# Sparse-layer front with half-width convolution matmuls and rows shared with GpSimd, and a transposing add in the recurrent layer, in a four-layer block on one core

## The chip, the cores and the metric

One core of a Trainium2 chip runs the whole program. The metric is the device time of one execution, in microseconds (us), lower is better. The engines are named as the profile names them: PE is TensorE, DVE is VectorE, ACT is ScalarE, POOL is GpSimd, SP is SyncE (here it only issues DMAs). PEld is TensorE's weight load.

## The reference

The input `x` is 4 batches of 1024 rows of 256 numbers, so 4096 rows, all in float32. Four layers are added to it in turn, each on a layer-normalised copy of `x`:

```python
x = x + lru(layernorm(x))        # linear recurrent unit
x = x + ffn(layernorm(x))        # sparse feed-forward layer
x = x + attention(layernorm(x))  # 8 heads, latent keys and values
x = x + ffn(layernorm(x))        # the same sparse layer, same weights
```

Of the recurrent unit the last part matters here: `out` is its output before a small two-layer net, and it computes `y = gelu(out @ w1 + b1) @ w2 + b2 + out`, then a layer norm of `y`.

The sparse layer needs two gates (`so` and `si`). Each gate begins with what the reference calls a convolution: the 256 normalised columns are taken in 64 groups of 4, and each group is reduced to one number with its own 4 weights.

```python
xc = einsum('ngf,gf->ng', x2d.reshape(n, 64, 4), conv_w) + conv_b   # n = 4096 rows
mean, var = over all n rows                                          # batch norm
xa = gelu((xc - mean) * rsqrt(var + eps) * gamma + beta)
scores = softmax(xa @ lin_w.T + lin_b)    # then the top 32 of 256 are kept
```

The mean and variance run over all 4096 rows, so nothing behind them can begin before the last row's convolution is done. That part, from the normalised rows to the batch-norm statistics, is what is called the front of a sparse layer below.

## The kernel before

All 4096 rows of `x` stay in the on-chip memory. The work before the batch norm goes in 8 chunks of 512 rows, each of 4 tiles of 128 rows; the work behind it goes in 32 tiles. Each engine has its own program, written out by hand in the order in which it runs; engines meet only at semaphores.

**A chunk of a front.** (1) ACT writes four normalised tiles with one multiply-add each (`z_rows_of`, line 755), into one of two row buffers. (2) PE turns them by eight 128x128 transposes (`transposes`, line 1522) into two PSUM banks. (3) ACT copies the two banks to `zT` (`zT_chunk`, line 762), so that the 256 columns now lie on 2 x 128 partitions. (4) PE multiplies with the matrix `conv` (`feature_chunk`, line 1553): 256 inputs to 128 outputs, 64 of each gate, as two matmuls of 128x128 weights and 512 columns that add up in one bank. (5) DVE adds the bias into `xcT` (line 1303) and takes statistics (line 1306). The scale and shift of a row's norm (`rs`) come from DVE's statistics and four small POOL instructions (`next_rstd`, lines 576 to 584). `conv` is mostly zeros: the first 128 columns of a row feed only the first 32 groups of each gate, the other 128 only the last 32.

The first sparse layer's front (f = 0) is woven into the last two steps of the recurrent layer; its last chunk needs the last residual of that layer. The second one's front (f = 1) stands by itself behind the attention layer, in `ffn(1)` of ACT, PE, POOL and DVE.

**A step of the recurrent layer** (`lru_step`, 8 of them) runs on PE in a fixed order: input products, transposes two chunks ahead, the mixing matmuls (line 1574), more input products (line 1535), `w1` (line 1589), input products again, and then the `w2` group (lines 1602 and 1604): for each of 4 tiles, two matmuls of 256 columns with `w2`, and then `out` is added to the same sums by two ordinary matmuls with the identity, which turn it back to rows. The group waits for both halves of the gelu (`l_y1`, ACT line 831):

```python
for k in range(KB2):
    mm(o, y1T[:, k, js], w2[:, k, :], start=k == 0, stop=False)
for k in range(KB2):
    last = mm(o[:, k * P:k * P + P], outT2[:, k, js], ident[:, :], start=False,
              stop=k == KB2 - 1)
```

**Set-up.** SP issues the weights' DMAs one after another (line 486), then the other chunks of `x` (line 490). POOL spreads the convolution's weights into a masked array (line 603), DVE sums it to `conv` (line 1296), and ACT copies the turned gate weights into `lin` (lines 798 and 799).

## Time and profile before

| | |
|---|---|
| median of 3 runs | 1435.57 us (1435.55 to 1437.32) |
| profiled execution, own time | 1435.77 us |
| profiled execution, span | 1434.1 us |
| PE busy | 1236.0 us (86%) |
| DVE busy | 1185.6 us (83%) |
| ACT busy | 1104.1 us (77%) |
| POOL busy | 982.3 us (69%) |

The span reaches from the first to the last instruction of the program; 1.7 us of the execution lie around it. PE's busy time overstates its work, since a matmul's record includes the time in which its results drain; for the rate of a series of matmuls one takes the distance of their starts. A float32 matmul of the program is two MATMUL records, a float32 transpose is one. The recurrent layer with the woven-in front takes the first 296 us, the sparse layer behind it runs to about 500 us, attention to 1204 us, and the second sparse layer to the end.

### The profile page before, as it was taken

The numbers are of one execution on the slowest core, as the hardware profiler recorded it, in microseconds if no ns is written. First come the engines' busy times: TensorE is split into PE (matmuls) and PEld (weight loads), VectorE is DVE, ScalarE is ACT, GpSimd is POOL, SyncE is SP. The second block draws the span as 40 slices with busy tenths as digits, with TensorE's granted clock in tenths as the row PEclk, the third lists the DMA queues.
The fourth block names the chain that finished last, engine by engine and source line by source line (L and its number), as shares of the span: only waits on it lengthen the run. The fifth ranks groups of instructions, "written<-read, shape, count | busy, mean of one in ns | idle before, by whom it ended". The sixth has DMA issues, their size and how long they took to land.

```text
span 1434.1 us, 31009 instructions
## 1 busy us (share of the span) xinstructions
PE 1236.0 (86%) x10236; PEld 762.0 (53%) x10236; DVE 1185.6 (83%) x3173; ACT 1104.1 (77%) x2487; POOL 982.3 (69%) x1109
## 2 busy tenths in 40 slices
PE   3899999866777688999999999999999999677775
PEld 2455545434444435565666666666666667344443
DVE  6999999469999978777887778877778853699997
ACT  3232332678899769999999998999998986898886
POOL 4355753248788867777777677777777771288887
PEclk9899999969899999999999999999999999899998
DMA  7100000000000000000000000000000000000000
GB/s 196 44 1 1 1 0 1 0 1 1 1 1 1 1 1 2 2 3 2 2 2 3 2 2 1 3 2 2 2 2 2 2 2 1 0 16 31 21 25 30
DMA packets 26427, 14.84 MB, mean 10 GB/s; under 512 B 14422, under 2 KB 26012, under 8 KB 26268
## 3 DMA queue, kind: packets, MB, share of 16 engines
q1 hardware_dynamic: 26268, 12.87, 3.4%
q8 instruction: 82, 1.34, 0.4%
q14 instruction: 77, 0.63, 0.1%
HBM read 8.60 MB, written 4.19 MB: 9 GB/s over the span
## 4 chain that ended last, share of the span: by engine, by line
PE 47%; DVE 19%; issue 16%; ACT 13%; POOL 4%; DVEq 0%; DMA 0%; SPq 0%; POOLq 0%; ACTq 0%
PE banks L1821 6%; PE banks L1823 5%; PE banks L1810 5%; DVE arena L1364 5%; ACT arena L1035 4%; DVE arena L1359 4%; PE banks L1771 3%; PE banks L1747 3%; PE banks L1839 3%; PE banks L1838 3%; PE banks L1840 3%; PE banks L1574 3%; ACT arena L1043 2%; POOL arena L713 2%; PE banks L1553 2%
## 5 line engine op out<-in xcount | busy, mean ns | idle before, releaser
L713 POOL TENSOR_TENSOR arena<-arena 128x512 f16<-128x512 f32 x384 | 441.1, 1166 | 156.5 <-ACT arena L1043 151.8
L1035 ACT ACTIVATE arena<-banks 128x512 f32<-128x512 f32 x512 | 304.5, 600 | 53.5 <-PE banks L1823 49.8
L1438 DVE TENSOR_REDUCE arena<-banks 128x1 f32<-128x512 f32 x512 | 327.4, 680 | 8.9 <-PE banks L1810 5.9
L1043 ACT ACTIVATE arena<-arena 128x512 f16<-128x512 f32 x512 | 316.2, 633 | 0.0
L1838 PE MATMUL banks<-arena 128*128 128x65 f16 x2048 | 214.4, 193 | 6.2 <-POOL arena L713 5.8
L1839 PE MATMUL banks<-arena 128*128 128x64 f16 x2048 | 214.5, 195 | 0.0
L1840 PE MATMUL banks<-arena 128*128 128x65 f16 x2048 | 213.6, 192 | 0.0
L1838 PEld LDWEIGHTS banks<-arena 128*128 128x128 f16 x2048 | 190.9, 96 | 35.4 <-issue 9.4
L1462 DVE TENSOR_TENSOR arena<-arena 128x512 f16<-128x512 f32 x128 | 106.5, 832 | 124.7 <-ACT arena L1043 124.3
L1364 DVE MATCH_REPLACE8 arena<-arena 128x256 f32<-128x256 f32 x512 | 205.7, 409 | 1.1 <-issue 0.8
L1821 PE MATMUL banks<-arena 128*128 128x512 f16 x512 | 194.1, 379 | 14.3 <-ACT arena L1035 12.8
L1839 PEld LDWEIGHTS banks<-arena 128*128 128x128 f16 x2048 | 190.2, 97 | 28.3
L1359 DVE MAX8 arena<-arena 128x8 f32<-128x256 f32 x512 | 190.2, 413 | 14.1 <-ACT arena L879 9.6
L1810 PE MATMUL banks<-arena 128*128 128x512 f16 x512 | 193.8, 380 | 4.6 <-DVE arena L1438 4.6
L1823 PE MATMUL banks<-arena 128*128 128x512 f16 x512 | 193.8, 378 | 0.0
L1840 PEld LDWEIGHTS banks<-arena 128*128 128x128 f16 x2048 | 190.3, 99 | 0.0
L1699 PE MATMUL banks<-fW,arena 128*128 128x256 f32 x256 | 79.8, 438 | 42.2 <-ACT arena L926 42.2
L1810 PEld LDWEIGHTS banks<-arena 128*128 128x128 f16 x512 | 57.8, 113 | 71.3 <-DVE arena L1438 11.9
L1821 PEld LDWEIGHTS banks<-arena 128*128 128x128 f16 x512 | 50.4, 98 | 58.0 <-ACT arena L1035 35.9
L1699 PEld LDWEIGHTS banks<-fW,arena 128*128 128x128 f32 x256 | 46.4, 201 | 61.8 <-ACT arena L926 57.7
L1686 PE MATMUL banks<-fW,arena 128*128 128x256 f32 x256 | 79.0, 439 | 0.0
L1678 PE MATMUL banks<-lin,arena 128*128 128x512 f32 x128 | 72.6, 651 | 4.8 <-ACT arena L951 4.8
(197 smaller groups left out, 2670.0 us busy)
## 6 DMA issues: line engine op xcount, KB each, us to landing
x<-in_L_attn_a_x SPq DMA_DIRECT2D x8, 512.0 KB, 3.9
out<-x SPq DMA_DIRECT2D x8, 512.0 KB, 2.9
arena<-arena SPq DMA_DIRECT2D x64, 1.0 KB, 1.9
arena<-in_L_attn_a_W_in SPq DMA_DIRECT2D x1, 768.0 KB, 5.7
arena<-in_L_attn_a_W_mid SPq DMA_DIRECT2D x1, 512.0 KB, 7.5
arena<-in_L_attn_a_w_w SPq DMA_DIRECT2D x2, 256.0 KB, 8.0
arena<-in_L_attn_b_Wq SPq DMA_DIRECT2D x1, 512.0 KB
arena<-in_L_attn_b_Wo SPq DMA_DIRECT2D x1, 512.0 KB
```

Source lines behind the costliest of these rows:

```text
L713: nc.gpsimd.tensor_tensor(pr_lo[c][:, kt, :], pr[:, kt, :], pr_hi[c][:, kt, :], ALU.subtract).then_inc(a_lP, 1)
L1035: nc.scalar.activation(pr[:, kt, :], ps[6 + kt % 2][:, :], ACT.Exp, scale=SM_SCALE).then_inc(a_P, 1)
L1043: nc.scalar.activation(pr_hi[c][:, kt, :], pr[:, kt, :], ACT.Copy).then_inc(a_hi, 1)
L1359: nc.vector.max(m8[p][:, i, r, :], src).then_inc(f_k[i], 1)
L1364: nc.vector.match_replace(wk[p][:, i, r % 2, :], m8[p][:, i, r, :], src, TAKEN).then_inc(f_k[i], 1)
L1438: nc.vector.tensor_reduce(mx_half[c][:, i // 2, i % 2:i % 2 + 1], ps[n % MAX_BANKS][:, :], X, ALU.max).then_inc(a_mx, 1)
L1810: mm(ps[n % MAX_BANKS][:, :], every[:, j, :], kA[B % 2][:, half * CH:half * CH + CH], start=True, stop=True).then_inc(a_mps, 1)
L1821: mm(o[:, :], kA[B % 2][:, kt * P:kt * P + P], qA[:, slot, c * CH:c * CH + CH], start=True, stop=False)
L1823: mm(o[:, :], kB[B % 2][:, kt * P:kt * P + P], qB[:, slot, c * CH:c * CH + CH], start=False, stop=True).then_inc(a_sps, 1)
L1838: mm(o, pr_hi[c][:, kt, js], lat[B % 2][:, kt, 0:1 + HD], start=kt == 0, stop=False)
L1839: mm(o[:, 1:1 + HD], pr_hi[c][:, kt, js], lat[B % 2][:, kt, 1 + HD:], start=False, stop=False)
L1840: last = mm(o, pr_lo[c][:, kt, js], lat[B % 2][:, kt, 0:1 + HD], start=False, stop=kt == KT - 1)
```

## The change

Three edits and what goes with them.

1. **Convolution.** The outputs are laid out anew: partitions 0 to 63 hold groups 0 to 31 of both gates, partitions 64 to 127 groups 32 to 63. `conv` becomes two blocks of 64 columns. Instead of two 128-column matmuls that add up, there are two matmuls with 64 weight columns, one per half of the inputs, each writing its own half of the bank's partitions. With the layout go the weights' DMAs (4 and 12 small ones for 2 and 6), the masked array (128 columns for 256), and ACT's copies into `lin` (4 for 2 per half).
2. **Rows.** In the whole second front and in the last two chunks of the first, ACT writes two of the four normalised tiles and POOL the other two (`half_rows`); PE waits for both (`s_zh`).
3. **Recurrent layer.** `out` is added by transposing matmuls (`is_transpose=True`) into the running sums, between the two `w2` matmuls of a tile, and PE waits for the second half of the gelu only before the first tile's second `w2` matmul.

```diff
-        conv = sb("conv", [P, KB2, P])
+        conv = sb("conv", [P, KB2, HD])
...
+        QUAD = HD // 2
...
-            (lin_n[:, :, 0:HD], so_lin_w.rearrange("(k p) g -> p k g", p=P)),
-            (lin_n[:, :, HD:P], si_lin_w.rearrange("(k p) g -> p k g", p=P)),
-            (bnp[0:HD, 0:1], so_conv_b.rearrange("(g a) -> g a", a=1)),
...
+        ] + [(lin_n[:, :, QUAD * q:QUAD * q + QUAD],
+              (so_lin_w, si_lin_w)[q % 2].rearrange("(k p) g -> p k g", p=P)[:, :, QUAD * (q // 2):QUAD * (q // 2) + QUAD])
+             for q in range(4)] + [
+            (bnp[QUAD * q:QUAD * q + QUAD, i:i + 1],
+             pair[q % 2].rearrange("(g a) -> g a", a=1)[QUAD * (q // 2):QUAD * (q // 2) + QUAD, :])
+            for i, pair in enumerate(((so_conv_b, si_conv_b), (so_gamma, si_gamma), (so_beta, si_beta)))
+            for q in range(4)
...
+            def half_rows(of, dst, turns):
+
+                pool.wait_ge(s_tps, turns)
+                for j in (2, 3):
+                    last = nc.gpsimd.tensor_scalar(dst[:, j, :], x[:, of * TPC + j, :], rs[:, of * TPC + j, 0:1],
+                                                   rs[:, of * TPC + j, 1:2], ALU.mult, ALU.add)
+                last.then_inc(s_zh, 1)
+
             over_chunks(pool, lru_step)
             rstd2(NCH - 1)
             residual(NCH - 1)
+            pool.wait_ge(n_p, 4 * (NCH - 1))
+            half_rows(NCH - 2, front_row[0], 2 * (LN_FFN1 + NCH - 3))
...
             next_rstd((NCH - 1) * TPC, NCH - 1, TPC)
+            pool.wait_ge(n_p, 4 * NCH)
+            half_rows(NCH - 1, front_row[1], 2 * (LN_FFN1 + NCH - 2))
             ffn(0)
...
-            for chunk in range(NCH - 3, NCH):
-                rstd_of("out", chunk)
+            for n in range(NCH):
+                if n == 2:
+                    rstd_of("out", NCH - 3)
+                    rstd_of("out", NCH - 2)
+                if n == 4:
+                    rstd_of("out", NCH - 1)
+                pool.wait_ge(n_p, 4 * group_of["out", n] + 4)
+                half_rows(n, z_rows[n % 2], 2 * (LN_FFN2 + n - 1) if n > 1 else 2 * LN_FFN2)
...
-                z_rows_of(m, front_row[m % 2])
+                z_rows_of(m, front_row[m % 2], 2 if m >= NCH - 2 else TPC)
...
-                for k in range(KB2):
-                    last = mm(ps[xc_bank(f, n)][:, :], conv[:, k, :], zT[n % 2][:, k, :], start=k == 0,
-                              stop=k == KB2 - 1)
+                for k in range(KB2):
+                    last = mm(ps[xc_bank(f, n)][HD * k:HD * k + HD, :], conv[:, k, :], zT[n % 2][:, k, :],
+                              start=True, stop=True)
...
-                pe.wait_ge(l_y1, n * 2 + 2)
+                pe.wait_ge(l_y1, n * 2 + 1)
...
+                    mm(o, y1T[:, 0, js], w2[:, 0, :], start=True, stop=False)
                     for k in range(KB2):
-                        mm(o, y1T[:, k, js], w2[:, k, :], start=k == 0, stop=False)
-                    for k in range(KB2):
-                        last = mm(o[:, k * P:k * P + P], outT2[:, k, js], ident[:, :], start=False,
-                                  stop=k == KB2 - 1)
+                        mm(o[:, k * P:k * P + P], outT2[:, k, js], ident[:, :], start=False, stop=False,
+                           is_transpose=True)
+                    if j == 0:
+                        pe.wait_ge(l_y1, n * 2 + 2)
+                    last = mm(o, y1T[:, 1, js], w2[:, 1, :], start=False, stop=True)
```

How instructions stand on PE in a `w2` group and in the woven-in front behind it (names: `arena` holds the recurrent layer's and the row buffers, `zrow` is the other row buffer). Before, two of the four tiles of the last group and what follows:

```order
L1602 MATMUL banks<-arena 128x256 x2
L1604 MATMUL banks<-ident,arena 128x128 x2
L1602 MATMUL banks<-arena 128x256 x2
L1604 MATMUL banks<-ident,arena 128x128 x2
L1522 MATMUL banks<-ident,zrow 128x128 x8
L1553 MATMUL banks<-zT,conv 128x512 x2
L1522 MATMUL banks<-ident,arena 128x128 x8
```

Now:

```order
L1624 MATMUL banks<-arena 128x256
L1626 MATMUL banks<-ident,arena 128x128 x2
L1630 MATMUL banks<-arena 128x256
L1624 MATMUL banks<-arena 128x256
L1626 MATMUL banks<-ident,arena 128x128 x2
L1630 MATMUL banks<-arena 128x256
L1543 MATMUL banks<-ident,zrow 128x128 x8
L1576 MATMUL banks<-zT,conv 64x512 x2
L1543 MATMUL banks<-ident,arena 128x128 x8
```

The two turning matmuls now stand between the two `w2` matmuls, and the convolution's two matmuls write 64 partitions each; the number of operations is the same.

POOL's program at the end of the recurrent layer (L564, now L565, is the last residual; L576 to L584, now L577 to L585, is `next_rstd` of the last chunk). Before:

```order
L564 TENSOR_TENSOR x<-x,arena 128x1024
L576 TENSOR_TENSOR nve<-nmv,eps_c 128x4
L577 TENSOR_TENSOR nnm<-nmv,minus_one 128x4
L581 TENSOR_TENSOR rs<-nve,minus_half 128x4
L584 TENSOR_TENSOR rs<-nnm,rs 128x4
L638 TENSOR_SCALAR bn_var<-bmv 128x1
```

Now:

```order
L565 TENSOR_TENSOR x<-x,arena 128x1024
L635 TENSOR_SCALAR zrow<-x,rs 128x256 x2
L577 TENSOR_TENSOR nve<-nmv,eps_c 128x4
L578 TENSOR_TENSOR nnm<-nmv,minus_one 128x4
L582 TENSOR_TENSOR rs<-nve,minus_half 128x4
L585 TENSOR_TENSOR rs<-nnm,rs 128x4
L635 TENSOR_SCALAR arena<-x,rs 128x256 x2
L649 TENSOR_SCALAR bn_var<-bmv 128x1
```

The rows of chunk 6 stand ahead of the last chunk's scale and shift, those of chunk 7 behind them. In the second front POOL writes two tiles for each of the 8 chunks, with the last chunk's scale and shift between chunks 3 and 4:

```order
L635 TENSOR_SCALAR zrow<-x,rs 128x256 x2
L635 TENSOR_SCALAR arena<-x,rs 128x256 x2
L577 TENSOR_TENSOR nve<-nmv,eps_c 128x4
L578 TENSOR_TENSOR nnm<-nmv,minus_one 128x4
L582 TENSOR_TENSOR rs<-nve,minus_half 128x4
L585 TENSOR_TENSOR rs<-nnm,rs 128x4
L635 TENSOR_SCALAR zrow<-x,rs 128x256 x2
```

Before, POOL had the three chunks' scales and shifts there and nothing else.

## Rows read from the trace of the kernel before

**Rows 1.** The page: busy time of the engines

```profile
PE 1236.0 (86%) x10236; PEld 762.0 (53%) x10236; DVE 1185.6 (83%) x3173; ACT 1104.1 (77%) x2487; POOL 982.3 (69%) x1109
```

**Rows 2.** Timeline, DVE: start, length, operation, [idle before, who ended it]

```profile
99.38 1.41 DVE L1206 SCALAR_TENSOR_TENSOR arena<-banks,arena 128x512 f32<-128x512 f32 x2 [0.34 <-PE banks L1535]
101.02 1.41 DVE L1206 SCALAR_TENSOR_TENSOR arena<-banks,arena 128x512 f32<-128x512 f32 x2 [0.23 <-PE banks L1535]
...
168.74 1.78 DVE L1296 TENSOR_REDUCE conv<-xcT 128x64 f32<-128x256 f32 x4
```

**Rows 3.** Timeline, PE, last four steps of the recurrent layer

```profile
186.65 3.67 PE L1535 MATMUL banks<-zT,arena 128*128 128x512 f32 x8 [2.03 <-DVE arena L1206]
...
242.08 1.13 PE L1602 MATMUL banks<-arena 128*128 128x256 f32 x4 [0.78 <-ACT arena L831]
243.05 0.61 PE L1604 MATMUL banks<-ident,arena 128*128 128x128 f32 x4
243.49 1.03 PE L1602 MATMUL banks<-arena 128*128 128x256 f32 x4
...
258.61 1.88 PE L1553 MATMUL banks<-zT,conv 128*128 128x512 f32 x4
260.33 1.04 PE L1522 MATMUL banks<-ident,zrow 128*128 128x128 f32 x8
261.20 1.02 PE L1589 MATMUL banks<-arena 128*128 128x512 f32 x2
...
267.64 1.07 PE L1522 MATMUL banks<-ident,arena 128*128 128x128 f32 x8 [1.11 <-ACT arena L755]
```

**Rows 4.** Timeline, POOL, then PE and DVE, end of the first front

```profile
279.13 2.00 POOL L564 TENSOR_TENSOR x<-x,arena 128x1024 f32<-128x1024 f32 x1 [2.56 <-ACT arena L776]
283.73 0.20 POOL L576 TENSOR_TENSOR nve<-nmv,eps_c 128x4 f32<-128x4 f32 x1 [2.61 <-DVEq L1156]
...
288.66 5.30 PE L1553 MATMUL banks<-zT,conv 128*128 128x512 f32 x8
...
280.36 0.75 DVE L1303 TENSOR_SCALAR xcT<-banks,bnp 128x512 f32<-128x512 f32 x1 [2.13 <-PE banks L1553]
...
281.75 1.39 DVE L1142 BATCH_NORM_STATS2 nst<-x 128x6 f32<-128x256 f32 x4
```

**Rows 5.** Timeline, ACT, PE and DVE, second front

```profile
1206.26 2.06 ACT L755 ACTIVATE zrow<-x,rs 128x256 f32<-128x256 f32 x4
1208.23 1.06 ACT L762 ACTIVATE zT<-banks 128x512 f32<-128x512 f32 x2
1209.18 2.07 ACT L755 ACTIVATE arena<-x,rs 128x256 f32<-128x256 f32 x4
...
1204.14 1.04 PE L1522 MATMUL banks<-ident,zrow 128*128 128x128 f32 x8
...
1227.72 0.75 DVE L1303 TENSOR_SCALAR xcT<-banks,bnp 128x512 f32<-128x512 f32 x1 [0.24 <-PE banks L1553]
```

**Rows 6.** Two stretches: length, busy of PE, PEld, DVE, ACT, POOL, granted clock

```profile
288.60:294.00 5.40, 5.40 (x13) 2.26 (x10) 1.46 (x3) 1.88 (x4) 0.00 (x0) 0.68 0.00 0
1205.40:1228.00 22.60, 22.45 (x90) 11.79 (x90) 11.63 (x22) 20.54 (x44) 1.56 (x4) 1.00 0.00 1
```

**Rows 7.** Groups by shape, POOL: the one-input operations: busy, mean ns of one

```profile
L683 POOL TENSOR_SCALAR arena<-arena 64x512 f16<-64x512 f16 x64 | 49.1, 767 | 5.3
...
L596 POOL TENSOR_SCALAR arena<-arena 128x512 f32<-128x512 f32 x2 | 4.0, 2010 | 0.1
```

**Rows 8.** Timeline, PE, set-up: 16 records in two partition halves

```profile
41.93 2.22 PE L1642 MATMUL banks<-arena 64*64 64x256 f32 x16
```

**Rows 9.** Timeline, SP, POOL and PE, set-up

```profile
17.66 0.60 SPq L486 DMA_DIRECT2D bnp<-in_L_ffn_si_beta  x1
...
28.86 1.57 POOL L603 TENSOR_SCALAR_AFFINE_SELECT xcT<-xcT 128x256 f32<-128x256 f32 x4
...
60.61 2.08 PE L1574 MATMUL banks<-arena 128*128 128x512 f32 x2 [5.29 <-DVE arena L1240]
```

More of the change, by code:

```diff
@@ L253, in hybrid_block_kernel @@
         s_z = sem("s_z")
+        s_zh = sem("s_z_half_chunk_pool")
         s_tps = sem("s_zT_psum")
@@ L602, in _ @@
                 for i in range(2):
-                    nc.gpsimd.affine_select(out=cvs[:, k, i, :], in_=cvb[:, i, :],
-                                            compare_op=ALU.is_equal, fill=0.0, base=-P * k,
-                                            pattern=[[1, D]], channel_multiplier=-1).then_inc(s_prep, 1)
+                    nc.gpsimd.affine_select(out=cvs[:, k, i, :], in_=cvb[:, i, k * P:k * P + P],
+                                            compare_op=ALU.is_equal, fill=0.0, base=0,
+                                            pattern=[[1, P]], channel_multiplier=-1).then_inc(s_prep, 1)
             add_ln_bias(0)
@@ L748, in _, with z_rows_of @@
             nc.scalar.activation(trig, ang_n, ACT.Sin).then_inc(s_act0, 1)
-            def z_rows_of(of, dst):
+            def z_rows_of(of, dst, rows=TPC):
                 act.sem_inc(s_turn, 1)
-                for j in range(TPC):
+                for j in range(rows):
                     t = of * TPC + j
@@ L797, in _ @@
                 act.wait_ge(s_pe0, k + 1)
-                nc.scalar.activation(lin[0:HD, k * P:k * P + P], ps[4 + k][0:HD, 0:P], ACT.Copy)
-                nc.scalar.activation(lin[HD:P, D + k * P:D + k * P + P], ps[4 + k][HD:P, 0:P],
-                                     ACT.Copy).then_inc(s_ev0, 1)
+                for q in range(4):
+                    at = slice(QUAD * q, QUAD * q + QUAD)
+                    last = nc.scalar.activation(lin[at, D * (q % 2) + k * P:D * (q % 2) + k * P + P],
+                                                ps[4 + k][at, 0:P], ACT.Copy)
+                last.then_inc(s_ev0, 1)
             for k in range(KB2):
@@ L1295, in conv_matrix @@
                 for k, i in ((0, 0), (0, 1), (1, 0), (1, 1)):
-                    link(nc.vector.tensor_reduce(conv[:, k, i * HD:i * HD + HD],
+                    link(nc.vector.tensor_reduce(conv[:, k, i * QUAD:i * QUAD + QUAD],
                                                  cvs[:, k, i, :].rearrange("p (g f) -> p g f", f=4), X, ALU.add))
@@ L1542, in front_turn @@
                     pe.wait_ge(f_xc, m - 1)
+                if m >= NCH - 2:
+                    pe.wait_ge(s_zh, m - NCH + 3)
                 transposes(LN_FFN1 + m, front_row[m % 2], 2 * (m % 2))
@@ L1709, in ffn @@
                     for n in range(2):
+                        pe.wait_ge(s_zh, 3 + n)
                         transposes(LN_FFN2 + n, z_rows[n], 2 * n)
@@ L1713, in ffn @@
                         if n + 2 < NCH:
+                            pe.wait_ge(s_zh, 5 + n)
                             transposes(LN_FFN2 + n + 2, z_rows[n % 2], 2 * (n % 2))
```

13 lines of the change are left out of this document (4 added, 9 removed).

## The prediction

> **What bounds the kernel now.** The page's busy times come first: PE 86%, DVE 83%, ACT 77%, POOL 69% [rows 1]. No engine carries the whole span, so each stage is read by itself, for the wait that ends last there. POOL is the least busy, but in the recurrent layer it writes residuals and scales that others wait for.
>
> The timelines of the recurrent layer show two regimes. In the first four steps PE finds DVE busy: it stands idle 2.03 us for `L1206` at 186.65 [rows 3], and of PE DVE waits only 0.34 and 0.23 us a step [rows 2]. From there PE runs nearly without a gap, so in the last four steps its instructions are the time.
>
> At the end of that layer the chain is serial: the last convolution of DVE's queue, `L1303` at 280.36, stands ahead of the last chunk's statistics, `L1142` at 281.75, and those ahead of POOL's scale and shift at 283.73 [rows 4]. The last two convolutions then run at a clock of 0.68 on average between 288.6 and 294 (a mix of 2.4 and 1.2 GHz) and take 5.30 us for eight records [rows 4, 6].
>
> The second front is ACT-bound in a steady beat: rows 2.06 us, copies 1.06 us, one chunk start to the next 1209.18 - 1206.26 = 2.92 [rows 5]. PE follows at granted clock 1.00 [rows 6]. PE is near its own limit there: eight transposes and four convolution records.
>
> **The transposing add.** A pair of 256-column `w2` matmuls (four records) takes about 0.87 us, the four 128-column records of the identity 243.49 - 243.05 = 0.44 [rows 3]. A transpose is one record: eight take 261.20 - 260.33 = 0.87, so 0.109 each [rows 3]. Two in place of four records save 0.22 a tile, 0.87 a group of four tiles. Steps 4 to 7: 4 x 0.85 = 3.4 (a little taken off for changes of mode). Steps 0 to 3 are DVE's, where PE's lead is worth only what DVE waits for it, 0.34 + 0.23 = 0.57 in all [rows 2]. Sum 4.0. No row shows a transpose into a running sum. Its bounds are 0.109 (a plain one) and 0.22 (no saving); I take 0.109, since nothing in the rows makes a transpose's time depend on its bank.
>
> **The split wait.** PE stands idle 0.78 for the gelu's second half at 242.08 [rows 3]. Now the first half and the tile's turning matmuls (0.43 + 0.22) stand ahead of it, which cover nearly all: 0.7. Behind the wait stand only the rest of the group and the chunks after it, which wait now as well.
>
> **The convolution, in halves.** A chunk takes 260.33 - 258.61 = 1.72, four records of 0.43 [rows 3]. The new matmuls have as many columns, so the count of records is the same; time falls only if the two, on separate column halves of the array, run side by side. The nearest row is `L1642` in set-up: 16 records of 256 columns on 64x64 parts in 2.22 us, where 16 x 0.87 / 4 = 3.5 would be their time one by one [rows 3, 8]. Side by side here: 2 x 0.43 = 0.86, and I put 0.3 on top for two changes between full and half tiles (an estimate; bounds 0 and 0.6): 1.16, saving 0.56.
>
> What that is worth, chunk by chunk: the first two lie on PE's path, 1.1. The third's gain goes into the wait for ACT's rows behind it, 1.11 [rows 3]. The next ones hide behind ACT, but for the sixth: DVE's `L1303` waits 2.13 for it and `L1142` stands behind, so 0.5 (more is held back by POOL's residual, which ends at 281.13) [rows 4]. The last two drop from 5.30 to about 3.9: two pairs at the slow clock and two changes; 1.4. The sum over the bias row `conv`, `L1296`, takes 4 x 0.43 on DVE in the DVE-bound part, and reads half as much: about 0.5 of 1.78 [rows 2].
>
> **POOL's rows.** `half_rows` issues two 128x256 operations with a scale and a shift per partition. No row shows it. The nearest is `L596`, also float32 with a per-partition scalar, but 512 columns: 2.01 us [rows 7]. Its small fixed part is about 0.2 (the 128x4 operation at 283.73 [rows 4]), so by columns 256 take 0.2 + 0.9 = 1.1. The lower bound is `L683`, with constants and half the partitions, 0.77 for 512 columns, so 0.48; the upper is `L596`'s whole 2.01 [rows 7]. I take **1.1**, by the row that is nearest in kind.
>
> In the first front: chunk 6's rows start after the residual (281.13) and end about 281.2 + 2.2 + 0.1 = 283.5, and the last scale and shift, which would now be due at 283.2, come 0.3 late. Chunk 7's take 2.2 + 0.1 for its hand-over, where ACT took 2.06 for four: a loss of 0.2. ACT's two end at 1.0, unused. Together -0.5.
>
> Sum of the first front and the recurrent layer: 4.0 + 0.7 + 1.1 + 0.5 + 1.4 + 0.5 - 0.5 = **7.7**.
>
> The Trainium skill speaks to this price ("GPSIMD Engine Reference", § 3.1): an elementwise loop at about 1.8 cycles an element at best, 769 ns for 512 elements. `L683` agrees, 767 ns; `L596`, 2010 ns for as many, doesn't. By the page a row costs about 0.4 us and the total would come out some 4 us lower, about 1420.
>
> **The second front.** ACT now has 2 x 0.52 + 1.06 = 2.1 a chunk, PE 0.87 + 1.16 + a little = 2.1, POOL 2 x 1.1 = 2.2. So POOL sets the beat, narrowly. Chunks 0 and 1 are written before attention ends; chunk 2's rows need the first chunk's transposes done, 1204.14 + 0.87 + hand-over = 1205.2 [rows 5]. Six chunks from there take 13.2, the last scale and shift between them 1.7 (a 1.0 us power and small ones), to 1220.1. Then the last transposes 1.0, copies 1.1 and convolution 1.2: DVE's last bias at about 1223.6 against 1227.72 [rows 5]. Gain **4.1**. The new wait `s_zh` stands on PE ahead of each chunk's transposes; behind it wait the previous chunk's convolution and DVE's add, which the times above include.
>
> **Set-up, nothing.** SP issues eight more small DMAs at 0.60 [rows 9], 4.8 us, so the last weights come about 28, POOL's `L603` (28.86 now) up to some 2 us later, the other chunks of `x` 4.8 later, and ACT has four copies more, about 1. PE has 5.29 idle before 60.61, for DVE [rows 9]; that is the cover. Gone, it would cost up to 2; and POOL's later work may meet other DVE work: 1 either way.
>
> Together 7.7 + 4.1 = 11.8. The sum is made against the profiled execution's 1435.77 (span 1434.1 plus 1.7), 0.2 over the median: **1424.0**.
>
> **Rivals.**
>
> *The halves do not overlap* (the change does not do what it says). For: both read the same 128 input rows with different moving data, which `L1642`'s 64-row parts don't. A chunk then takes 1.72 + 0.3 = 2.0. In the first front the 3.0 of the convolution become about -0.7; in the second PE's beat is 0.87 + 2.0 = 2.9, as now, minus 0.5 at the edges. 1435.8 - 4.0 + 0.5 = 1432.3.
>
> *POOL's row costs 2.0*, with the price per instruction, not per column: **slower**. Place: the six chunks of the second front (12 operations) and four operations' worth in the first, so 16 us lost for each us of price over 1.1; the change is even at 1.1 + 11.8 / 16 = 1.84. At 2.01 it is 1424.0 + 14.6 = 1438.6. Against: `L683` and the 128x4 rows show that time goes with columns. For: `L596` is the only row of this kind.
>
> *POOL's row costs 0.5.* The beat falls to PE's 2.1 and scale and shift no longer count: 2.1 less; the last chunk of the first front 1.3 and chunk 6's 0.3 less: about 1420.4.
>
> *The clock falls in the second front.* The clock is 1.00 there, but 0.68 at the end of the first front [rows 6], where PE had waited between its chunks. With POOL as bound, PE waits a little in each beat. At 1.2 GHz the transposes 1.74 and the pairs 1.9 make a beat of 3.7, and the second front loses 5.7 where it gained 4.1: 1433.8. The Trainium skill has a rule on that ("TensorE: Matmul & The Clock Gate", Part 4): transposes in transpose mode don't count as busy for the clock. By that rule the shorter convolutions leave less that counts; in the trace, 64 transposes between 32 convolution records kept 1.00, so it has not decided there so far.
>
> *The transposing add is a two-pass operation*: 3.4 less, 1427.4.
>
> **How the numbers follow.** Chances: forecast, with POOL's price from 0.8 to 1.5, 0.50; POOL cheap 0.16; no overlap 0.12; transposing add 0.04; POOL at 2.0 0.08; clock 0.05; other, both signs, 0.05. The likeliest gives **1424.0**; its own range is 1420.5 to 1430.5 (16 us for each us of the price up to 1.5, less of it down to 0.8, where PE bounds the beat; changes of mode 0 to 0.6 and set-up 1 lie within). The range to hold 8 in 10 goes from the cheap POOL to the halves in series, 1419.5 to 1432.5; outside are the slower clock, the expensive row and the unnamed. 0.2% is 2.9 us, about what a measurement of this kernel tells from no change. Faster by more (below 1432.7): 0.50 + 0.16 + 0.04 + most of no overlap, 0.10, and 0.03 of the rest: **0.83**. Same: 0.02 + 0.05 + 0.02 + 0.01 at the even point of POOL's price: **0.10**. Slower: **0.07**.
>
> **What would show it.** In the profile after: the tile of `w2` 1.1 us for 1.31; the convolution's pair 1.2 a chunk, two records starting nearly together; POOL's row 1.1; in the second front a beat of 2.2 with PE's idle time ended by POOL's rows; no clock below 1.00 there; the start of attention some 7.7 us earlier. The forecast is wrong if PE's transposes there wait on ACT or follow without a gap (POOL cheap), if four convolution records still take 1.7 or more, if the beat is over 2.9, or if the first steps of the recurrent layer start later than they did.

## The result and the profile after

The changed kernel takes **1421.35 us**, median of 4 runs (1419.80 to 1424.02), where the kernel before took 1436.44 (4 runs, 1435.55 to 1437.54): ratio 0.9897, 95% interval 0.9877 to 0.9916, so 15 us less (12 to 18). The forecast was 1424.0, range 1419.5 to 1432.5, faster with 0.83. The profiled execution is the fastest of the four, 1419.80 with a span of 1418.1. It is set against the profiled one before, of 1435.77: 16.0 less.

The page of the changed kernel; PE's busy time is 17 us less, POOL's 10 more [rows 1]:

```profile
PE 1219.2 (86%) x10172; PEld 746.1 (53%) x10172; DVE 1183.4 (83%) x3173; ACT 1094.3 (77%) x2471; POOL 992.4 (70%) x1129
```

**Where the 16 us came from.** DVE issues the same 3173 instructions in the same order in both kernels, so its starts can be laid side by side. Five stretches cover the span; each is the difference of two starts (the ends of it are DVE's first `SCALAR_TENSOR_TENSOR` of the recurrent layer, DVE's last bias of each front, and PE's first transposes of the second front):

| stretch | before, us | after, us | gained | forecast |
|---|---|---|---|---|
| set-up, to the first DVE work of the recurrent layer | 35.61 | 33.30 | 2.3 | 0 |
| recurrent layer and first front | 258.38 | 251.13 | 7.3 | 7.7 |
| first sparse layer and attention | 910.15 | 909.46 | 0.7 | 0 |
| second front | 23.58 | 16.55 | 7.0 | 4.1 |
| second sparse layer behind it | 206.38 | 207.66 | -1.3 | 0 |

The third and fifth hold none of the changed work; they show what such a stretch varies by. Over the profiled executions of all fourteen kernels of this document they take 908.9 to 911.2 and 205.5 to 207.9 us.

**Set-up.** The timeline of DVE before, in the piece that the forecast priced at nothing (start, length, operation):

```profile
30.50 2.08 DVE L1192 SCALAR_TENSOR_TENSOR arena<-arena 128x128 f32<-128x128 f32 x1
...
35.61 0.75 DVE L1206 SCALAR_TENSOR_TENSOR arena<-banks,arena 128x512 f32<-128x512 f32 x1
```

And after, DVE, then POOL:

```profile
29.85 0.35 DVE L1213 SCALAR_TENSOR_TENSOR arena<-arena 128x128 f32<-128x128 f32 x1
...
33.30 1.41 DVE L1227 SCALAR_TENSOR_TENSOR arena<-banks,arena 128x512 f32<-128x512 f32 x2
...
32.04 1.50 POOL L604 TENSOR_SCALAR_AFFINE_SELECT xcT<-xcT 128x128 f32<-128x128 f32 x4 [3.29 <-DMA xcT<-in_L_ffn_si_lin_b]
33.52 1.99 POOL L550 TENSOR_TENSOR x<-x,arena 128x1024 f32<-128x1024 f32 x1
```

One instruction of DVE's table chain took 2.08 us where its like takes 0.35 to 0.48. POOL's first 1024-column addition of `x` stood beside it, at 30.41 before. Such a pair, a POOL addition and a DVE operation side by side of which one or both take longer than alone, is called a meeting below. Now POOL waits 3.29 us for the weights, with eight more DMAs issued ahead, and its addition falls behind DVE's chain. The forecast had seen POOL start later, and put what would come of it at "1 either way".

**The recurrent layer.** The timeline of PE, after:

```profile
183.23 5.37 PE L1556 MATMUL banks<-zT,arena 128*128 128x512 f32 x8 [3.59 <-DVE arena L1227]
...
188.43 0.59 PE L1624 MATMUL banks<-arena 128*128 128x256 f32 x2
188.86 0.38 PE L1626 MATMUL banks<-ident,arena 128*128 128x128 f32 x2
...
189.52 0.59 PE L1624 MATMUL banks<-arena 128*128 128x256 f32 x2
...
252.94 1.08 PE L1576 MATMUL banks<-zT,conv 128*64 128x512 f32 x4
253.94 1.09 PE L1543 MATMUL banks<-ident,zrow 128*128 128x128 f32 x8
```

A tile of the `w2` group takes 189.52 - 188.43 = 1.09 us for 1.31; the two turning records take 0.22. From the convolution's four records to the transposes behind them it is 253.94 - 252.94 = 1.00 us for 1.72 [rows 3]. But PE now waits longer for DVE, 3.59 for 2.03, and the eight records behind that wait take 5.37 us for 3.67.

The stretches of the changed kernel with their granted clock (length, busy of PE, PEld, DVE, ACT, POOL, clock) tell why:

```profile
183.00:188.40 5.40, 5.17 (x8) 2.20 (x9) 5.40 (x7) 0.00 (x0) 0.57 (x1) 0.68 0.01 3
278.10:284.40 6.30, 5.08 (x18) 2.49 (x18) 2.76 (x4) 3.21 (x7) 0.85 (x2) 0.62 0.00 0
1193.90:1209.80 15.90, 15.90 (x98) 8.45 (x96) 11.57 (x22) 14.82 (x30) 8.02 (x16) 1.00 0.00 1
```

The clock was 0.68 in the first of them, a mix of 2.4 and 1.2 GHz; the same eight records ran at 1.00 before. That gives back 1.7 us, and it goes with the longer wait: behind 3.58 to 3.59 us of waiting for DVE these eight records took 5.1 to 5.4 us in all eight kernels profiled here that have that wait, all of them with the transposing add, and 3.67 in the three whose wait was 2.03 to 2.34, none of them with it. At the end of the first front the clock is 0.62 now, where it was 0.68 in rows 6.

The end of the first front on POOL, after:

```profile
273.88 1.10 POOL L635 TENSOR_SCALAR zrow<-x,rs 128x256 f32<-128x256 f32 x2
276.04 0.20 POOL L577 TENSOR_TENSOR nve<-nmv,eps_c 128x4 f32<-128x4 f32 x1 [1.05 <-DVEq L1177]
```

Two rows take 1.10 us together, **0.555 each** where the forecast took 1.1. Chunk 6's rows end before the last scale and shift is due, so they delay nothing.

The 7.3 us of this stretch so fall into four pieces: 1.1 less up to PE's wait for DVE (183.23 - 33.30 = 149.93 us for 186.65 - 35.61 = 151.04), 1.7 more for the clock behind it, 5.5 less from there to the fifth chunk's transposes (78.12 us for 83.62, forecast 5.2), and 2.3 less from those to DVE's last bias (17.88 for 20.21, forecast 1.4).

**The second front.** PE, then POOL and DVE, after:

```profile
1193.89 1.04 PE L1543 MATMUL banks<-ident,zrow 128*128 128x128 f32 x8
...
1195.73 1.08 PE L1576 MATMUL banks<-zT,conv 128*64 128x512 f32 x4
1196.74 1.09 PE L1543 MATMUL banks<-ident,zrow 128*128 128x128 f32 x8
1197.76 1.08 PE L1576 MATMUL banks<-zT,conv 128*64 128x512 f32 x4
...
1202.07 1.09 POOL L635 TENSOR_SCALAR zrow<-x,rs 128x256 f32<-128x256 f32 x2 [0.94 <-PE banks L1543]
...
1210.44 0.73 DVE L1324 TENSOR_SCALAR xcT<-banks,bnp 128x512 f32<-128x512 f32 x1
```

The beat is 1197.76 - 1195.73 = 2.03 us for 2.92 [rows 5]: 1.01 for the convolution's records and 1.02 for the eight transposes. PE has no gap in it, and POOL waits 0.94 for PE before each of its last two pairs of rows: PE is the bound, with ACT close behind (one copy to the next in 1.94). The front ends at 1210.44, where the kernel before was at 1227.72 [rows 5].

### The profile page after: what moved, and what is told of

It is laid out like the page before. It is cut to its first block, busy times and chain, and to the rows that moved or that the text cites. A ratio compares the mean times of both kernels' runs of the same rounds, so it can differ in the third digit from the quotient of the medians.

```text
span 1418.1 us, 30913 instructions
## 1 busy us (share of the span) xinstructions
PE 1219.2 (86%) x10172; PEld 746.1 (53%) x10172; DVE 1183.4 (83%) x3173; ACT 1094.3 (77%) x2471; POOL 992.4 (70%) x1129
## 4 chain that ended last, share of the span: by engine, by line
PE 43%; DVE 22%; issue 17%; ACT 13%; POOL 4%; DVEq 0%; DMA 0%; SPq 0%; POOLq 0%; ACTq 0%
PE banks L1848 6%; PE banks L1850 5%; DVE arena L1385 5%; PE banks L1837 5%; DVE arena L1380 4%; ACT arena L1056 4%; PE banks L1798 4%; PE banks L1774 3%; PE banks L1866 3%; PE banks L1865 3%; PE banks L1867 3%; ACT arena L1064 2%; DVE arena L1244 2%; DVE arena L1227 2%; POOL arena L726 2%
## 5 line engine op out<-in xcount | busy, mean ns | idle before, releaser
L781 ACT ACTIVATE zT<-banks 128x512 f32<-128x512 f32 x48 | 26.4, 601 | 64.6 <-PE banks L1543 64.6
```

## The experiments

Each kernel below was timed beside the kernel before on the same chip, whose median was 1436.24, 1436.72 and 1436.35 in three sittings. The changed kernel's own ratio is 0.9897 [0.9877, 0.9916]. "More" and "less" are differences of medians to its 1421.35, unless another kernel is named; they are good to about 3 us. Line numbers are those of the changed kernel unless an experiment shifts them by some lines.

### Without POOL's rows

ACT writes all four tiles; `half_rows`, its calls and `s_zh` are gone.

```diff
-                z_rows_of(m, front_row[m % 2], 2 if m >= NCH - 2 else TPC)
+                z_rows_of(m, front_row[m % 2])
...
-                        z_rows_of(n + 2, z_rows[c], 2)
+                        z_rows_of(n + 2, z_rows[c])
```

> The change without its second edit: ACT writes all four tiles of every chunk, POOL none. If POOL's rows carry the second front (theory), its beat returns to ACT's 2.9 us for 2.03, so some 6.5 us are lost there and about 1 at the last chunk of the first front: 1428 to 1430. Rival, that the shorter convolution alone sets the beat: at most 2 us lost, 1423.

Measured: 1427.42 us, ratio 0.9930 [0.9912, 0.9947], so 6.1 more than with them, just under the 1428 to 1430 expected. The timeline of its PE in the second front:

```profile
1202.70 1.09 PE L1524 MATMUL banks<-ident,zrow 128*128 128x128 f32 x8 [0.82 <-ACT zrow L755]
...
1205.62 1.09 PE L1524 MATMUL banks<-ident,arena 128*128 128x128 f32 x8 [0.82 <-ACT arena L755]
```

The beat is back at 2.92, and PE waits 0.82 for ACT in each. The second front takes 22.43 us, for 16.55 with POOL's rows and 23.58 before. So without POOL's rows the shorter convolution gives nothing to the beat, and 1.2 us at the two ends.

### Without the halves

The old layout, DMAs and two full-width matmuls that add up.

```diff
-                    last = mm(ps[xc_bank(f, n)][HD * k:HD * k + HD, :], conv[:, k, :], zT[n % 2][:, k, :],
-                              start=True, stop=True)
+                    last = mm(ps[xc_bank(f, n)][:, :], conv[:, k, :], zT[n % 2][:, k, :], start=k == 0,
+                              stop=k == KB2 - 1)
```

> The change without its first edit: convolution in two full-width matmuls, the old layout, the old DMAs of the weights. Theory of overlapping halves: PE's beat in the second front is 0.87 + 1.72 + about 0.15, 0.7 more for each of 8 chunks, 3 us more in the first front, 0.5 at the conv matrix: about +9, 1430. A second theory says that the eight more DMAs of the layout themselves gained 2.3 us in set-up, since POOL's first 1024-column addition starts behind DVE's table chain and not beside it: then this kernel's DVE L1206-type instruction in the first chunk starts near 35.6 again and not at 33.3, and the time is 1432. Rival, no such link: 33.3 stays.

Measured: 1427.15 us, 0.9932 [0.9915, 0.9948]: 5.8 more, well under the 1430 expected, or 1432 with the link to set-up, which is borne out below. Its profiled run is its slowest, 1429.43. PE in the second front:

```profile
1206.52 1.04 PE L1541 MATMUL banks<-ident,arena 128*128 128x128 f32 x8
1207.39 1.88 PE L1574 MATMUL banks<-zT,conv 128*128 128x512 f32 x4
1209.11 1.04 PE L1541 MATMUL banks<-ident,zrow 128*128 128x128 f32 x8
```

The beat is 2.59, with no gap: 0.87 for the transposes and 1.72 for the convolution. All its matmuls are full tiles, so there is no change of tile size to pay, where the expectation had added 0.15. DVE's first work of the recurrent layer starts at 35.53 again, with a DVE operation of 2.08 us at 30.41 before it. The DMAs of the new layout and the set-up's 2.3 us are linked, as the second theory said.

### Both matmuls on one half

Both halves of the inputs go to the first 64 output partitions; the other 64 are not written, so half of the features are left out.

```diff
-                    last = mm(ps[xc_bank(f, n)][HD * k:HD * k + HD, :], conv[:, k, :], zT[n % 2][:, k, :],
-                              start=True, stop=True)
+                    last = mm(ps[xc_bank(f, n)][0:HD, :], conv[:, k, :], zT[n % 2][:, k, :],
+                              start=k == 0, stop=k == KB2 - 1)
```

> The change with both matmuls of the convolution on the same column half, one adding to the other (partitions 64 to 127 of the bank are not written, so half the features are left out of the computation). If the gain comes from the two halves running side by side, a chunk takes 1.72 plus up to 0.3 again where the change has 1.01: PE's beat in the second front is 2.8 to 3.0 for 2.03, 6 to 8 us lost there, 3 in the first front: +8 to +11, 1430 to 1432. If half-width matmuls are quicker by themselves, the beat stays near 2.0.

Measured: 1429.90 us, 0.9952 [0.9936, 0.9969]: 8.6 more.

```profile
1203.68 1.93 PE L1576 MATMUL banks<-zT,conv 128*64 128x512 f32 x4
1205.54 1.09 PE L1543 MATMUL banks<-ident,arena 128*128 128x128 f32 x8
1206.56 1.93 PE L1576 MATMUL banks<-zT,conv 128*64 128x512 f32 x4
```

The four records take 1205.54 - 1203.68 = 1.86, against 1.01 on two halves: the weights' width alone gives nothing. Two series of 0.43 fewer are 0.86, and 1.86 - 1.01 = 0.85. The gain is that the two halves run side by side, though they share all 128 input rows.

The change between full and half tiles shows here as well. The half-tile records take 0.14 more than four times 0.43 (1.86 for 1.72; in the changed kernel they take 0.15 more than twice 0.43, 1.01 for 0.86), and the eight transposes behind them take 1206.56 - 1205.54 = 1.02 for the 0.87 that they take between full-width matmuls in the kernel without the halves. A chunk has both changes, so it pays 0.15 + 0.15 = 0.30, and the changed kernel's beat is 0.87 + 0.86 + 0.30 = 2.03.

### The transposing add undone

```diff
-                        mm(o[:, k * P:k * P + P], outT2[:, k, js], ident[:, :], start=False, stop=False,
-                           is_transpose=True)
+                        mm(o[:, k * P:k * P + P], outT2[:, k, js], ident[:, :], start=False, stop=False)
```

> The change with ordinary matmuls in place of the transposing ones (same order, same split wait). Theory: each group of four tiles takes 0.87 us more, 3.4 in the last four steps and 0.5 in the first: +3.9, 1425. Rival, that transposing into a running sum takes two passes: no change.

Measured: 1423.96 us, 0.9908 [0.9891, 0.9924]: 2.6 more, where 3.9 was expected, with overlapping intervals. Set-up and second front are the same to 0.1 us as with it; the recurrent layer and first front are 5.1 longer in the profiled run. Its PE:

```profile
183.29 3.67 PE L1556 MATMUL banks<-zT,arena 128*128 128x512 f32 x8 [2.34 <-DVE arena L1227]
...
233.55 5.36 PE L1612 MATMUL banks<-arena 128*128 128x512 f32 x8
```

Two things are mixed in the 5.1. The four groups behind the wait take 0.9 more each, and 0.7 the one with the gelu's wait, 3.4 together, as forecast; ahead of them PE starts at 183.29 for 183.23, so the 0.5 expected there is not seen. The rest is the clock. Here PE waits only 2.34 us for DVE and its next eight records run at full speed, which saves the 1.7 that the changed kernel loses there. But the clock falls at two later places where it did not in the profile of the changed kernel, for about 1.7 us each: the eight records at 233.55 (3.71 there), and the transposes at 263.82 with the tile behind them. So the transposing add saves 3.4 us of PE's work here, and the longer wait for DVE gives 1.7 of it back; the 2.6 of the medians lies between 1.7 and 3.4.

### One wait for both halves of the gelu

```diff
-                pe.wait_ge(l_y1, n * 2 + 1)
+                pe.wait_ge(l_y1, n * 2 + 2)
```

> The change with the wait for both halves of the gelu ahead of the w2 group again. The forecast put the split at 0.7 us (one idle stretch of 0.78 in step 6): 1422, and PE's idle stretch for ACT's gelu of 0.7 to 0.8 is back in that step. Rival: the stretch was cover for a later wait and nothing changes, or other steps have it too now that PE reaches the group earlier: 1 to 2 us.

Measured: 1420.00 us, 0.9882 [0.9866, 0.9899], not to be told from the changed kernel. The idle stretch is back, in the one step where it was:

```profile
239.77 0.70 PE L1624 MATMUL banks<-arena 128*128 128x256 f32 x2 [0.78 <-ACT arena L852]
```

So the term is right in its place. It is somewhat smaller than 0.78, since in the changed kernel the group's first tile still takes 238.40 - 236.93 = 1.47 us for 1.09, and here 1.19: 0.5 net. That is too little for the runs to show: the runs of one kernel here lie 3 to 6 us apart.

### POOL's rows at twice the price

```diff
                 pool.wait_ge(s_tps, turns)
+                pool.wait_ge(s_spare, spent[0])
+                for j in (2, 3):
+                    nc.gpsimd.tensor_scalar(spare[:, j - 2, :], x[:, of * TPC + j, :], rs[:, of * TPC + j, 0:1],
+                                            rs[:, of * TPC + j, 1:2], ALU.mult, ALU.add).then_inc(s_spare, 1)
+                spent[0] += 2
```

> The change with POOL's price per chunk of rows doubled: two like operations into a spare buffer ahead of the two that count, so that a row costs 1.1 us as the forecast took it, where 0.555 was measured. If the forecast's sum was right but for that price, the second front's beat becomes POOL's 2.2, the last scale and shift counts, and the last two chunks of the first front end 1.3 to 1.6 later: +4 to +5, 1425 to 1426, near the 1424.0 forecast. Rival, that other terms were off and cancelled: the difference is under 2 or over 7.

Measured: 1425.58 us, 0.9929 [0.9913, 0.9946]: 4.2 more. The second front, PE and POOL:

```profile
1205.56 1.09 PE L1551 MATMUL banks<-ident,zrow 128*128 128x128 f32 x8 [1.73 <-POOL zrow L643]
...
1207.72 1.09 PE L1551 MATMUL banks<-ident,arena 128*128 128x128 f32 x8
...
1209.87 1.09 PE L1551 MATMUL banks<-ident,zrow 128*128 128x128 f32 x8
...
1207.63 1.11 POOL L639 TENSOR_SCALAR spare<-x,rs 128x256 f32<-128x256 f32 x2
1208.70 1.12 POOL L643 TENSOR_SCALAR zrow<-x,rs 128x256 f32<-128x256 f32 x2
```

The beat is POOL's, 2.15, and PE waits 1.73 where the last scale and shift stands between. From PE's first transposes, at 1196.13, to DVE's last bias, at 1215.58, it is 19.45 us: 4.1 less than the 23.58 before. That is the forecast's number for this front, to a tenth, once POOL's row costs what the forecast took it to cost. Against the changed kernel it is 2.9 more.

The 4.2 in all is no such match. In the profiled run the recurrent layer and first front are 1.7 longer (252.86 for 251.13), but that is lost before POOL's first row there: PE's convolution at 232.57 and the eight records behind it take 1.97 and 4.32 us where they took 1.08 and 3.71, by the clock. From the fifth chunk's transposes to DVE's last bias it is 17.92 for 17.88. The later rows do hold PE's transposes up by 1.1 (it waits 3.74 for 2.66), but the clock was higher at the end, 0.80 for 0.62. So the 1.3 to 1.6 expected there are not seen.

### The row that misled

The operation behind the 2.01 us is written in the form of the rows: product and sum, two scalars per partition, the same result.

```diff
-                nc.gpsimd.tensor_scalar(decT[:, k, :], decT[:, k, :], decay[:, k:k + 1], 0.0,
-                                        ALU.add, ALU.add).then_inc(s_decay, 1)
+                nc.gpsimd.tensor_scalar(decT[:, k, :], decT[:, k, :], decay[:, k:k + 1],
+                                        decay[:, k:k + 1], ALU.mult, ALU.add).then_inc(s_decay, 1)
```

> The change, with the 512-column operations of L597 (L596 of the kernel before: one scalar per partition, one constant, two additions, 2.01 us) written in the form of the rows: product and sum, both scalars per partition, same result. If the price goes by the form, they take 0.19 + 2 x (0.555 - 0.19) = 0.92 us; if by the place (DVE beside it) or the scalar, 2.0 again. The whole time does not tell, under 1 us either way.

The group of shapes on POOL, in the changed kernel and then in this one (busy, mean ns of one):

```profile
L597 POOL TENSOR_SCALAR arena<-arena 128x512 f32<-128x512 f32 x2 | 4.0, 2007 | 0.1
```

```profile
L597 POOL TENSOR_SCALAR arena<-arena 128x512 f32<-128x512 f32 x2 | 1.6, 783 | 0.1
```

Same columns, type and place: 2007 ns in one form, 783 in the other, where the expectation had 920. The price goes by the form. Whether it is the mixed scalars or the two additions stays open; the run changed both. One run took 1420.79 us in all.

### The kernel before with a later addition in set-up

```diff
+            pool.wait_ge(s_dve0, 1)
             add_ln_bias(0)
```

> The kernel before, and one wait more: POOL's first 1024-column addition (L549, at 30.41 in its trace) waits until DVE's chain of table doublings is done. Theory of the set-up gain: the two-input additions of both engines hold each other up, DVE L1192 took 2.08 us beside it where its like takes 0.35 to 0.48; without the meeting DVE's first work of the recurrent layer starts at 33.5 instead of 35.6 and the whole is about 2 us faster, 1434. Rival: the 2.3 us of set-up come from elsewhere (DMA landing times): no change, 1436.

Measured: 1434.93 us against 1436.72, ratio 0.9987 [0.9977, 0.9996]: 1.8 less, with nothing of the change in it.

```profile
30.33 0.34 DVE L1193 SCALAR_TENSOR_TENSOR arena<-arena 128x128 f32<-128x128 f32 x1
...
33.71 2.73 DVE L1207 SCALAR_TENSOR_TENSOR arena<-banks,arena 128x512 f32<-128x512 f32 x4
```

The instruction of 2.08 us takes 0.34, and the layer starts at 33.71 for 35.61. PE, at the end of the steps that DVE bounds:

```profile
183.67 3.67 PE L1536 MATMUL banks<-zT,arena 128*128 128x512 f32 x8 [2.33 <-DVE arena L1207]
```

That is 149.96 us behind DVE's start, for 151.04 in the kernel before. So with the later addition alone these steps are 1.1 us shorter too. The kernel without the transposing add has 149.99, the one without the halves 149.98, the changed one 149.93. How the 1.1 arises, no run singles out.

### A spare addition in the changed kernel's gap

```diff
+            pool.wait_ge(s_x, 32)
+            nc.gpsimd.tensor_tensor(spare[:, :, :], x[:, 0:TPC, :], x[:, 0:TPC, :], ALU.add)
             pool.wait_ge(s_w, N_W)
```

> The change, and a POOL addition of two 1024-column inputs into a spare buffer in the gap in which POOL waits for the weights (28.7 to 32.0), so that nothing of POOL's own work starts later. Theory: it meets DVE's chain, one or two of DVE's instructions there take 1.7 us longer, and the first work of the recurrent layer starts at 35 instead of 33.3: +2, 1423.5. Rival: POOL's work beside DVE's costs nothing: 1421.4.

Measured: 1424.69 us, 0.9919 [0.9903, 0.9936]: 3.3 more, where 2 was expected; the intervals overlap. DVE, then POOL:

```profile
28.74 1.93 DVE L1208 TENSOR_SCALAR arena<-arena 128x128 f32<-128x128 f32 x1
...
33.16 2.10 DVE L1214 SCALAR_TENSOR_TENSOR arena<-arena 128x256 f32<-128x256 f32 x1
...
28.70 1.89 POOL L603 TENSOR_TENSOR spare<-x 128x1024 f32<-128x1024 f32 x1
...
32.95 2.03 POOL L551 TENSOR_TENSOR x<-x,arena 128x1024 f32<-128x1024 f32 x1
```

Two meetings, each of 1.6 us or more on DVE: the first pushes the chain back until it meets the next addition too. The recurrent layer starts at 36.60. POOL's gap was free for POOL and not for DVE.

### Placed behind DVE's products

The changed kernel has such meetings in every step that DVE bounds. DVE, then POOL:

```profile
99.95 3.02 DVE L1253 TENSOR_TENSOR arena<-arena 128x1024 f32<-128x1024 f32 x1
...
112.57 3.02 DVE L1236 TENSOR_TENSOR arena<-arena 128x1024 f32<-128x1024 f32 x1
...
98.91 2.98 POOL L565 TENSOR_TENSOR x<-x,arena 128x1024 f32<-128x1024 f32 x1
...
111.51 3.00 POOL L550 TENSOR_TENSOR x<-x,arena 128x1024 f32<-128x1024 f32 x1
```

Their like take 1.21 on DVE and 2.0 on POOL when alone. In steps 1 to 4 (0 to 4 for the bias) both POOL additions now wait for DVE's turned-back products (`PLACED = 4`):

```diff
                 if behind:
+                    if n <= PLACED:
+                        pool.wait_ge(l_dve, (n + 1) * L_STEPS + L_STEPS)
                     residual(n - 1)
+                if ahead2 and n <= PLACED:
+                    pool.wait_ge(l_dve, (n + 1) * L_STEPS + L_STEPS)
+                    add_ln_bias(n + 2)
...
-                if ahead2:
+                if ahead2 and n > PLACED:
                     add_ln_bias(n + 2)
```

> The change, with two of POOL's 1024-column additions (residual and bias of x) in steps 1 to 4 of the recurrent layer put where DVE reads PSUM, behind its turned-back products, by a wait on DVE's count. Theory: each meeting of such an addition with a DVE product of 1024 columns costs DVE 1.5 to 1.8 us (3.02 for 1.21), two a step in the part that DVE bounds; without them 6 to 9 us less until PE becomes the bound, 1413 to 1416. Rival: PE is bound there too now, or the additions come late for ACT: under 2 us less, or more time.

Measured: **1414.18 us** (1412.03 to 1415.90), ratio 0.9849 [0.9831, 0.9866], clear of the changed kernel's interval: 7.2 us less than it, 22 less than the kernel before. DVE, then POOL:

```profile
101.25 1.22 DVE L1259 TENSOR_TENSOR arena<-arena 128x1024 f32<-128x1024 f32 x1
...
112.06 1.22 DVE L1242 TENSOR_TENSOR arena<-arena 128x1024 f32<-128x1024 f32 x1
...
104.81 2.00 POOL L566 TENSOR_TENSOR x<-x,arena 128x1024 f32<-128x1024 f32 x1 [8.32 <-DVE arena L1267]
106.77 2.00 POOL L551 TENSOR_TENSOR x<-x,arena 128x1024 f32<-128x1024 f32 x1
```

Both operations of DVE are at their time alone. PE's wait of 3.59 us for DVE is gone with them, and so is the fall of the clock behind it: of the 6.9 us by which the profiled run is ahead at the next `w2` group (148.28 us behind DVE's start for 155.13), 1.7 are the clock's. POOL's additions now lie beside DVE operations with one input in PSUM (104.65 to 107.3) and beside statistics, and neither side is slower.

### The last meeting removed as well

```diff
+                    if n <= PLACED:
+                        pool.wait_ge(l_dve, (n + 1) * L_STEPS + 6)
                     turned_back(n + 1, 1)
```

and the wait of set-up as above.

> The placed version (two POOL additions a step behind DVE's work), and two waits more: POOL's second turned-back product (L545) in steps 0 to 4 starts behind DVE's last scan, and the first addition of set-up behind DVE's table chain. Theory: the meeting that is left in the placed version, scan 3.3 for 1.26 us with the product 3.3 for 2.0, goes too, 2 us a step in DVE's part until PE is the bound: 3 to 6 less than 1414.2, 1408 to 1411. Rival: PE, which shows no idle time between 100 and 186 us in the placed version, is bound already: under 1 us less.

Measured: 1414.77 us, 0.9857 [0.9841, 0.9874]: no better than the placed version, the rival. DVE's last input product of the recurrent layer starts at 210.29 for 212.96, but PE, nearly without a gap in both from 101 to 186 us, reaches the same matmul only at 185.63 for 186.05. PE is the bound there. The clock took even that:

```profile
225.24 1.98 PE L1585 MATMUL banks<-zT,conv 128*64 128x512 f32 x4 [2.42 <-ACT zT L790]
```

These four records take 1.98 where the placed version's take 1.08, at a granted clock of 0.91 over 216 to 236 us (1.00 there).

### The kernel before, placed

The same placing and the later first addition, without the change.

> The kernel before with the same placing of the two additions a step and the later first addition of set-up. If PE is the next bound of the recurrent layer, the change's shorter w2 groups are worth more once DVE is relieved, and here the placing gains less than the 7.2 us that it gave the changed kernel, plus 1.8 for set-up: 1430 to 1432. If the placing gains its 7.2 whatever PE does, and set-up 1.8: 1427.5.

Measured: 1430.76 us against 1436.35, ratio 0.9960 [0.9942, 0.9978]: 5.6 less in all, and not 7.2 + 1.8 = 9.0. The stretch from 101 to 186 us there, as in rows 6:

```profile
101.00:186.00 85.00, 85.00 (x282) 47.11 (x281) 83.25 (x148) 28.20 (x53) 46.41 (x43) 1.00 0.00 1
```

PE is busy throughout, so PE binds, and its longer `w2` groups cap the gain. A part of the missing 3.4 us may be the clock: the kernel before had no fall behind its wait of 2.03 us, so the placing had no 1.7 to win back. With the placing the change is worth 1430.8 - 1414.2 = 16.6 us, without it 15.1; that difference lies within what the runs vary, so that the two help each other is not shown by the medians.

## Why the prediction was right, and where not

The range held the time, and the sign was right. But the case that happened is the cheap row, which had a chance of 0.16, and not the likeliest one. The median lies 2.7 below the forecast and the profiled run 4.2 below: 2.3 by set-up and 2.9 by the second front, against 0.4 the other way in the recurrent layer with the first front and 0.6 in the two stretches without changed work. Within the stretches some errors cancelled.

- **What bounds the kernel.** Right: without POOL's rows the second front's beat was ACT's 2.92 again, and nearly all of the gain lay in the two fronts and the recurrent layer, beside set-up.
- **The transposing add.** A tile saved 0.22 and a group 0.87, so the 3.4 of the last four steps is right. Two parts are not. The 0.6 for the first steps is not seen: PE starts behind DVE at 183.23 with the add and at 183.29 without. And the forecast had no term for the clock: PE reaches DVE's product earlier, waits 3.59 us for it, and loses 1.7 behind that wait. Forecast 4.0 as a whole, measured 2.6 by the medians. (By its own working the rival of two passes would have cost 4.0 too, and not 3.4.)
- **The split wait.** 0.78 of idle time gone in the one place, 0.5 net for 0.7; in the runs not measurable.
- **The convolution.** The halves overlap, so the rival that they don't is refuted by the run on one half. The 0.3 for two changes of tile size came from no row, but it is what the runs show, 0.15 at each change: a chunk takes 0.86 + 0.30 = 1.16, as forecast, and 0.15 of it lies in the transposes.
- **The first four steps.** The matrix's four sums took 4 x 0.286 for 4 x 0.43, so 0.5 less on DVE, as forecast. With the 0.6 of the transposing add that makes 1.1, and 1.1 was measured. But the kernel before with the later addition has it as well, and the kernels without the one or the other change keep it (149.96 to 149.99 us for 149.93). So with set-up shifted neither term adds anything, and the agreement is luck.
- **POOL's rows: the term that was mis-sized.** The forecast took 1.1 us, "by the row that is nearest in kind", `L596`. It measured 0.555, and the kernel with the price doubled gave 4.1 us for the second front, the forecast's term (whose steps, added up as written, end at 1223.4 and not 1223.6). So the rule of the sum was right and its price wrong. The row chosen was the farther one: it shared type and partitions but not the form of operation, and form is what cost 2007 against 783 ns. In the second front the wrong price was worth 2.9 us. The cheap-row rival (chance 0.16, 1420.4) is the case that happened, with a beat of 2.03 where it said 2.1.
- **The page that was set aside there** was closer. The Trainium skill ("GPSIMD Engine Reference", § 3.1) puts an elementwise body of at most two operations at 1.03 cycles an element. Here 256 columns took 555 ns and 512 took 783 in the same form, 0.89 ns a column, which at the page's 1.2 GHz is 1.07 cycles. Its best-loop figure of 769 ns for 512 is near the 783 as well. The 2007 ns of `L596` fit neither figure.
- **Set-up at nothing: wrong by 2.3 us.** The later addition was seen, its bound was put at "1 either way", and the meeting it escaped (2.08 for 0.48) was in the trace. Removing the meeting in the kernel before gave 1.8 us by itself (0.6 to 3.3); adding one to the changed kernel cost 3.3.
- **The clock.** The rival that it falls in the second front is refuted: 1.00 there. But it fell at another place, behind PE's longer wait for DVE (3.59 us), for 1.7 us, and no step of the forecast had that.

So the first front and recurrent layer come out at 7.3 for 7.7 only by cancellation: the clock took 1.7, while the stretch behind the fall gained 7.8 where the forecast's terms for it add up to 6.6.

The meetings are the rule of the Trainium skill ("SBUF — State Buffer", "Who interferes with whom"): DVE and GpSimd share one pair of ports as an exclusive lock, which a DVE operation with two inputs in SBUF holds against a GpSimd operation that reads SBUF. The traces agree with their sizes: the DVE operation of 3.02 us ends 1.1 behind the POOL addition beside it (102.97 and 101.89), about its time alone, and with one input in PSUM nothing is lost.

## What to carry to other kernels

Price an operation on GpSimd by a row of the same form (which operations, scalars or constants), and not only of the same shape: here two forms of one shape differ by a factor of 2.6. When a change moves work of DVE or GpSimd in time, look at what each piece lies beside before and after; a two-input addition in the wrong microsecond cost more than the term one was arguing about, and placing two additions a step (7.2 us) added about half of what the whole change had given (15.1). Shorter work only counts until the next engine binds, so take away DVE's meetings and PE's records together. And an engine that is made faster ahead of another's work waits longer for it; look at what the clock does behind that wait.

## What the hardware showed unexpectedly

- Two matmuls of 128 input rows and 64 output columns each, with different moving data, run side by side on the two column halves: 1.01 us for four records of 512 columns, 1.86 on one half.
- A change between full and half tiles costs 0.15 us in each direction: the half-width records take 1.01 for 0.86, and the eight full transposes behind them 1.02 for the 0.87 that they take between full-width matmuls.
- A 128x128 float32 transpose into a running sum takes 0.11 us, as a plain one.
- A POOL operation with one scalar and one constant, both additions, took 2007 ns for 512 float32 columns; product and sum with two scalars took 783 ns there, and 555 ns for 256 columns.
- A one-input float32 DVE operation with both sides in SBUF was held up by a POOL addition as well: 1.93 us for 0.28 (`L1208` in the kernel with the spare addition).
- The clock fell for some microseconds behind PE's wait of 3.58 to 3.59 us for DVE in all eight kernels profiled that had it (0.68 over 183.0 to 188.4 us in the changed kernel, eight records in 5.37 us), and not in the three where the same wait was 2.03 to 2.34 (3.67 us).
- Behind a wait of 2.42 us for ACT it fell in some executions and not in others: the same four records took 1.98 and 1.08 us in the two placed versions. This is part of why executions of one kernel lie 3 to 6 us apart; what decides it stays open.
